# Weights times values of the first network: 64x128 half-array matmuls instead of 64x64 quarters

## Chip, core and metric

The kernel runs on one core of one Trainium2 chip. The metric is the device time of an execution in microseconds; less is better. The core has a matmul engine (TensorE, PE in the profile, with its weight loads listed apart as PEld), VectorE (DVE), ScalarE (ACT), GpSimd (POOL), and a sync engine (SP) that issues most DMAs.

## What is computed

32 records of 64 tokens with 256 dims go through two networks. The first has two cross-attention layers and an MLP; the second is one attention layer and an MLP, and is not touched here. A layer of the first network, cut to what matters:

```python
B, Q, S1, S2 = (4, 32, 256, 256); D, H, K, F = (256, 16, 128, 1024)   # shapes given: batch 32, 64 queries, 64 keys
qh = (q_in @ wq + bq).reshape(b, q_len, H, K)
kh = (kv_in @ wk + bk).reshape(b, t, H, K);  vh = (kv_in @ wv + bv).reshape(b, t, H, K)
kh = concatenate([kh, bias_k]); vh = concatenate([vh, bias_v])       # a 65th key
weights = softmax(einsum('bqhk,bthk->bhqt', qh, kh) / sqrt(K))
ctx = einsum('bhqt,bthk->bqhk', weights, vh).reshape(b, q_len, H * K)
return ctx @ wo + bo
```

The change is in the `ctx` line: per record and head, 64 queries x 64 keys of weights times 64 keys x 128 dims of values.

## The kernel before

Tokens are taken 128 at a time, so that the 128 partitions hold two records (b = 0 on partitions 0 to 63, b = 1 on 64 to 127). A layer is cut into 32 units: 8 pairs of heads (HP) times 4 groups of 512 tokens (G; 4 tiles of 128 tokens, GT). Two layers make 64 units. Each engine runs the same list of slots (`slots`, L248); a slot holds the front of one unit and the back of the unit before it, so a unit is worked on in two successive slots. The order on each engine is written out by hand, and semaphores join the engines.

TensorE's slot (L354 to L453) is, in this order: projections of Q and K (L377, `three`: each product in three fp32r matmuls of 128x128 by 512 columns, L168 to L170); the first half of V, `values(0)` (L387, 12 fp32r matmuls by 256 columns); for the unit before, weights times values (L404); the second half of V, `values(1)`; the scores (L433, plain fp32, stationary QT, moving KT, 65 columns for 64 keys and the bias key); for the unit before, the output projection (L447, 24 fp32r matmuls by 256 columns) of CHI and CLO.

The softmax of a unit lies on VectorE and ScalarE between its scores and its L404 one slot later: maximum (L606), subtraction (L615), exp (L524, ScalarE), sum (L567), reciprocal (L569), product (L571), and eight 32x32-block transposes (L578) that give PRT: 64 keys of record b on partitions b*64 and up, by (head, tile) j, by 64 queries. GpSimd adds to V the difference of bias rows (L332), so that the 65th key needs no row of its own.

The L404 stage: j runs over 8 (2 heads x 4 tiles), b over 2 records. The stationary operand is V (keys of record b x dims of head h), the moving operand is PRT (keys x 64 queries), the result stands in PSUM bank 3 + b, with dims on the partitions and j*64 to (j+1)*64 as columns. Both are plain fp32, which the trace shows as two matmul records and two weight loads per instruction. Before the stage TensorE waits for V (v_shift), PRT (pt_out) and for VectorE to have read banks 3 and 4 (x_settled). Behind it: ScalarE copies each bank to CHI (L513, waits for c_done), VectorE subtracts to get CLO (L596), and the output projection waits for CLO (c_lo). It writes into banks 3 and 4 again; VectorE adds those to X (L625).

Of the kernel before, what the change touches and what calls it, by code (L numbers as in the profile page):

```python
# [13 lines left out]
B, S, D = 32, 64, 256  # L14
TOK = B * S
P = 128
NT = TOK // P
DC = D // P
H, K = 16, 128
# [3 lines left out]
GT = NT // G  # L23
# [21 lines left out]
def program(nc, x, ctx_in, mask, wall, vrow, borow, vech, vecm, b_fc2, qw, kw, vw, ow, out_b, w1, w2, b2, out):  # L45
    es = ExitStack()
    with es:
        def sem(name):
            return es.enter_context(nc.semaphore(name))

        def sb(name, shape, dt=F32, scope=es):
            return scope.enter_context(nc.sbuf_tensor(name, shape, dt))

        bank = [es.enter_context(nc.psum_tensor(f"bank{i}", [P, 512], F32)) for i in range(5)]
# [111 lines left out]
        def three(e, dst, a_hi, a_lo, b_hi, b_lo, start, stop, **kw):  # L166

            e.matmul(dst, a_hi, b_hi, start=start, stop=False, **kw)  # L168
            e.matmul(dst, a_hi, b_lo, start=False, stop=False, **kw)  # L169
            return e.matmul(dst, a_lo, b_hi, start=False, stop=stop, **kw)  # L170
# [16 lines left out]
        with ExitStack() as ph:  # L187
# [13 lines left out]
            V = [sb(f"V{a}", [P, GT, 256], scope=ph) for a in range(2)]  # L201
# [8 lines left out]
            PRT = sb("PRT", [P, 2 * GT, S], scope=ph)  # L210
# [22 lines left out]
            c_done, o_done = sem("c_done"), sem("o_done")  # L233
# [28 lines left out]
            with nc.Block() as block:  # L262
# [90 lines left out]
                def _(e):  # L353
                    def slot(L, n, at, pair, hp, last):  # L354
# [4 lines left out]
                        if front:  # L359
# [6 lines left out]
                            for j, half, done, free in ((0, 1, q_done, v_out), (1, 0, k_done, k_out)):  # L366
# [5 lines left out]
                                for h in range(2):  # L372
# [3 lines left out]
                                    for c in range(DC):  # L376
                                        i = three(e, PROJ[2 * j + h][:, :], WHI[a][:, j, c, h * K:(h + 1) * K],  # L377
                                                  WLO[a][:, j, c, h * K:(h + 1) * K], SRC_HI[:, half, c, toks],
                                                  SRC_LO[:, half, c, toks], c == 0, c == DC - 1)
# [14 lines left out]
                        if back:  # L394

                            e.wait_ge(v_shift, 2 * n)
                            e.wait_ge(pt_out, n)
                            e.wait_ge(x_settled, 2 * n)
                            for j in range(2 * GT):
                                h, p = j // GT, j % GT  # L400
                                for dims in (slice(0, S), slice(S, P)):
                                    for b in range(2):
                                        keys = slice(b * S, (b + 1) * S)
                                        i = e.matmul(bank[3 + b][dims, j * S:(j + 1) * S],  # L404
                                                     V[(at - 1) % 2][keys, p, h * K + dims.start:h * K + dims.stop],
                                                     PRT[keys, j, :], start=True, stop=True)
                                        if j == 2 * GT - 1 and dims.start:
                                            i.then_inc(c_done, 1)
                        if front:
                            values(1)  # L410
                        if at == 0:
# [3 lines left out]
                        if front:  # L415
# [7 lines left out]
                            if last and at == G - 1:  # L423
# [3 lines left out]
                                for c in range(DC):  # L427
                                    e.matmul(logits[:, c, 384:512], ones[:, :], acc[L][:, c * P:(c + 1) * P],
                                             start=True, stop=True)
                            for h in range(2):  # L430
                                for q in range(GTOK // S):
                                    p, b = q // 2, q % 2
                                    i = e.matmul(logits[b * S:(b + 1) * S, h, p * KEYS:(p + 1) * KEYS],  # L433
                                                 QT[:, h, q * S:(q + 1) * S], KT[:, h, q, :], start=True, stop=True)
# [4 lines left out]
                        if back:  # L439

                            e.wait_ge(c_lo, 2 * n)
                            for j in range(2):
                                for p in range(2):
                                    ts = slice((2 * j + p) * P, (2 * j + p + 1) * P)
                                    dst = bank[3 + j][:, p * 256:(p + 1) * 256]
                                    for h in range(2):
                                        i = three(e, dst, CHI[:, h, ts], CLO[:, h, ts], WHI[ab][:, 3, h, :],  # L447
                                                  WLO[ab][:, 3, h, :], h == 0, h == 1)
# [12 lines left out]
                    for g in range(G):  # L461
# [7 lines left out]
                        for c in range(DC):  # L469
                            for p in range(GT):  # L470
                                i = e.transpose(CB[g % 2][c][:, p * P:(p + 1) * P], cin[g % 2][:, p, c * P:(c + 1) * P],
                                                ident[:, :])
# [7 lines left out]
                    for L in range(0, NL):  # L480
                        slots(e, L, slot)
# [849 lines left out]
```

## Time and profile before

| | |
|---|---|
| median of 3 runs | 1415.94 us (1415.51 to 1418.8) |
| profiled execution | 1415.35 us, span 1413.2 us |
| busy: PE | 1334.0 us (94%), 14427 matmul records |
| busy: PEld | 1189.8 us (84%) |
| busy: DVE, ACT, POOL | 904.8 (64%), 611.8 (43%), 587.3 us (42%) |
| L404, matmuls | 4096 records, 76.0 us busy |
| mean granted TensorE clock | 0.976 |

How to read it: the profile is of one execution. The span runs from its first to its last instruction. Busy time of a group of small matmuls is time in which any of them was under way, so overlapping ones aren't counted twice. A matmul record's length includes the time through the array; in a dense stream records overlap, and the distance between their starts is what one costs. A granted clock of 1.00 is 2.4 GHz, 0.50 is 1.2 GHz.

### The profile page before, as it was taken

What the parts mean: (1) busy time and instruction counts of PE and PEld (TensorE: products, weight loads), DVE (VectorE), ACT (ScalarE), POOL (GpSimd) and SP (SyncE); (2) the same over time, 40 slices, a digit from 0 to 9 for tenths busy, and PEclk for the clock granted to TensorE, in tenths of its full rate; (3) what the DMA queues carried; (4) which work ended last, traced back from release to release, by engine and by line L of the source; (5) the groups of instructions that cost most, each with busy time, mean ns of one, the idle gap of its engine ahead of it and who ended that gap; (6) DMA issues with size and microseconds to landing.
All of it is one profiled execution on the core that took longest, in us unless ns stands there. A gap on an engine that the chain in (4) does not pass through costs nothing. (4 is left out here: it accounts for less than half of the span.)

```text
span 1413.2 us, 33171 instructions
## 1 busy us (share of the span) xinstructions
PE 1334.0 (94%) x14427; PEld 1189.8 (84%) x14427; DVE 904.8 (64%) x1792; ACT 611.8 (43%) x1045; POOL 587.3 (42%) x521
## 2 busy tenths in 40 slices
PE   3999999999999799999999999987998999997898
PEld 3898888888888688888888888977887989996787
DVE  6567767676767866767666767685323588886322
ACT  3534343434444554343434444364223256665421
POOL 4524334144144543414414324364651055554654
PEclk8999999999999999999999999997999999998999
DMA  7011011011010101101101011000000000002000
GB/s 241 4 36 39 1 39 39 1 38 39 1 39 2 38 1 39 39 2 38 38 2 39 2 38 38 2 1 27 1 1 8 1 2 2 2 2 64 4 31 30
DMA packets 31764, 35.91 MB, mean 25 GB/s; under 512 B 955, under 2 KB 29187, under 8 KB 31619
## 3 DMA queue, kind: packets, MB, share of 16 engines
q1 hardware_dynamic: 31394, 33.70, 7.6%
q8 instruction: 114, 1.87, 0.6%
q14 instruction: 30, 0.25, 0.1%
q10 hardware_dynamic: 226, 0.10, 0.0%
HBM read 31.70 MB, written 2.10 MB: 24 GB/s over the span
## 5 line engine op out<-in xcount | busy, mean ns | idle before, releaser
L332 POOL TENSOR_TENSOR V<-V,DV 128x512 f32<-128x512 f32 x128 | 164.0, 1281 | 534.5 <-ACT V L500 534.5
L168 PE MATMUL bank<-SRC_HI,WHI 128*128 128x512 f32 x576 | 230.2, 400 | 4.3 <-PEq L262 4.3
L169 PE MATMUL bank<-SRC_LO,WHI 128*128 128x512 f32 x576 | 229.4, 398 | 0.0
L170 PE MATMUL bank<-SRC_HI,WLO 128*128 128x512 f32 x576 | 228.8, 397 | 0.0
L578 DVE STREAM_TRANSPOSE PRT<-PR 32x256 f32<-32x256 f32 x512 | 223.2, 436 | 8.3
L596 DVE TENSOR_TENSOR CLO<-bank,CHI 128x512 fp32r<-128x512 f32 x128 | 82.4, 686 | 135.9 <-ACT CHI L513 135.9
L492 ACT ACTIVATE QT<-bank,PB 128x512 f32<-128x512 f32 x128 | 87.8, 688 | 177.8 <-PE bank L170 177.8
L168 PE MATMUL bank<-WHI,CHI 128*128 128x256 f32 x512 | 152.0, 297 | 4.4 <-DVE CLO L596 4.0
L168 PE MATMUL bank<-WHI,SRC_HI 128*128 128x256 f32 x512 | 150.4, 294 | 0.0
L170 PE MATMUL bank<-WHI,CLO 128*128 128x256 f32 x512 | 145.1, 283 | 0.7 <-issue 0.7
L169 PE MATMUL bank<-WLO,CHI 128*128 128x256 f32 x512 | 144.9, 283 | 0.0
L169 PE MATMUL bank<-WLO,SRC_HI 128*128 128x256 f32 x512 | 143.9, 281 | 0.0
L170 PE MATMUL bank<-WHI,SRC_LO 128*128 128x256 f32 x512 | 143.9, 281 | 0.0
L168 PEld LDWEIGHTS bank<-SRC_HI,WHI 128*128 128x128 f32 x576 | 109.5, 190 | 27.0 <-POOL SRC_LO L163 4.5
L170 PEld LDWEIGHTS bank<-SRC_HI,WLO 128*128 128x128 f32 x576 | 109.2, 190 | 26.4
L169 PEld LDWEIGHTS bank<-SRC_LO,WHI 128*128 128x128 f32 x576 | 109.6, 190 | 21.9
L496 ACT ACTIVATE KT<-bank,PB 128x512 f32<-128x512 f32 x128 | 88.4, 691 | 89.9 <-PE bank L170 89.9
L625 DVE TENSOR_TENSOR X<-X,bank 128x512 f32<-128x512 f32 x128 | 88.0, 687 | 57.9 <-PE bank L170 57.9
L500 ACT ACTIVATE V<-bank 128x512 f32<-128x512 f32 x128 | 76.5, 597 | 79.5 <-PE bank L170 79.5
L168 PEld LDWEIGHTS bank<-WHI,CHI 128*128 128x128 f32 x512 | 98.2, 192 | 9.7 <-DVE CLO L596 5.8
L168 PEld LDWEIGHTS bank<-WHI,SRC_HI 128*128 128x128 f32 x512 | 96.1, 188 | 7.2
L169 PEld LDWEIGHTS bank<-WLO,SRC_HI 128*128 128x128 f32 x512 | 96.5, 188 | 2.7
(170 smaller groups left out, 3009.7 us busy)
## 6 DMA issues: line engine op xcount, KB each, us to landing
W<-in_wall SPq DMA_DIRECT2D x18, 1024.0 KB, 5.6
VROW<-in_vrow SPq DMA_DIRECT2D x18, 256.0 KB, 6.1
V<-in_ctx SPq DMA_DIRECT2D x4, 512.0 KB, 5.8
X<-in_x SPq DMA_DIRECT2D x4, 512.0 KB, 6.8
mlp_w<-in_w SPq DMA_DIRECT2D x2, 1024.0 KB, 7.7
out<-X SPq DMA_DIRECT2D x4, 512.0 KB, 2.9
BO<-in_borow SPq DMA_DIRECT2D x1, 256.0 KB, 7.0
W<-in_qw SPq DMA_DIRECT2D x1, 256.0 KB, 4.3
```

Of the source, the lines that this page charges most:

```text
L168: e.matmul(dst, a_hi, b_hi, start=start, stop=False, **kw)
L169: e.matmul(dst, a_hi, b_lo, start=False, stop=False, **kw)
L170: return e.matmul(dst, a_lo, b_hi, start=False, stop=stop, **kw)
L332: e.tensor_tensor(vs, vs, DV[a][:, :].unsqueeze(1).to_broadcast([P, 2, 2 * K]), ALU.add).then_inc(v_shift, 1)
L492: e.activation(QT[:, h, :], PROJ[h][:, :], ACT.Identity, bias=PB[a][:, 0, h:h + 1]).then_inc(q_out, 1)
L496: e.activation(KT[:, h, :, 0:S], PROJ[2 + h][:, :].rearrange("p (q k) -> p q k", k=S), ACT.Identity, bias=PB[a][:, 1, h:h + 1]).then_inc(k ...
L500: e.activation(V[at % 2][:, 2 * j:2 * j + 2, :], PROJ[j][:, :].rearrange("p (t n) -> p t n", n=256), ACT.Copy).then_inc(v_out, 1)
L578: i = e.transpose(PRT[b * S + z:b * S + z + 32, :, y:y + 32], PR[b * S + y:b * S + y + 32, :, z:z + 32])
L596: e.tensor_tensor(of_batch(CLO, b), by_tile(b), of_batch(CHI, b).bitcast(F32), ALU.subtract).then_inc(c_lo, 1)
L625: e.tensor_tensor(xs, xs, bank[3 + j][:, :].rearrange("p (t n) -> p t n", n=256), ALU.add).then_inc(x_settled, 1)
```

## The change

The loop over two halves of the head dims is gone. One matmul now has all 128 dims of a head in its stationary operand (64 keys x 128 dims) and writes all 128 partitions of the bank. Record b still decides the rows and the bank. So there are 16 instructions a unit (32 records) instead of 32 (64 records). Operands, results, their places in SBUF and PSUM, and all other engines' code are the same; c_done is raised by the last matmul of each b, as before.

```diff
                             for j in range(2 * GT):
                                 h, p = j // GT, j % GT
-                                for dims in (slice(0, S), slice(S, P)):
-                                    for b in range(2):
-                                        keys = slice(b * S, (b + 1) * S)
-                                        i = e.matmul(bank[3 + b][dims, j * S:(j + 1) * S],
-                                                     V[(at - 1) % 2][keys, p, h * K + dims.start:h * K + dims.stop],
-                                                     PRT[keys, j, :], start=True, stop=True)
-                                        if j == 2 * GT - 1 and dims.start:
-                                            i.then_inc(c_done, 1)
+                                for b in range(2):
+                                    keys = slice(b * S, (b + 1) * S)
+                                    i = e.matmul(bank[3 + b][:, j * S:(j + 1) * S],
+                                                 V[(at - 1) % 2][keys, p, h * K:(h + 1) * K],
+                                                 PRT[keys, j, :], start=True, stop=True)
+                                    if j == 2 * GT - 1:
+                                        i.then_inc(c_done, 1)
```

## Rows read from the trace of the kernel before

**Rows 1.** Page: busy us, share of the span and instructions of each engine.

```profile
PE 1334.0 (94%) x14427; PEld 1189.8 (84%) x14427; DVE 904.8 (64%) x1792; ACT 611.8 (43%) x1045; POOL 587.3 (42%) x521
```

**Rows 2.** Windows (us, busy of each engine, then TensorE clock, DMA share, GB/s).

```profile
300.00:400.00 100.00, 99.87 (x1190) 88.73 (x1189) 69.93 (x127) 41.00 (x65) 32.89 (x29) 1.00 0.05 15
485.00:500.00 15.00, 6.97 (x92) 6.62 (x91) 10.98 (x31) 4.67 (x8) 5.33 (x3) 0.66 0.01 1
1200.00:1212.00 12.00, 12.00 (x157) 10.95 (x157) 9.67 (x26) 8.42 (x20) 6.03 (x8) 1.00 0.00 1
```

**Rows 3.** Waits of TensorE, 100:957 (who for whom: us in total, times, longest).

```profile
PE bank L404 <- DVE PRT L578: 12.0, 2, 6.0
...
PE bank L404 <- issue: 1.5, 1, 1.5
```

**Rows 4.** Timeline of TensorE (start us, length us, line, xcount), units at 534 and 548.

```profile
534.43 1.16 PE L404 MATMUL bank<-PRT,V 64*64 64x64 f32 x64
535.52 0.38 PE L168 MATMUL bank<-WHI,SRC_HI 128*128 128x256 f32 x1
...
535.86 0.28 PE L170 MATMUL bank<-WHI,SRC_LO 128*128 128x256 f32 x1
535.98 0.28 PE L168 MATMUL bank<-WHI,SRC_HI 128*128 128x256 f32 x1
...
548.27 1.16 PE L404 MATMUL bank<-PRT,V 64*64 64x64 f32 x64
```

**Rows 5.** By line: ns minimum/median/maximum, starts (x64, x4: 534:537 alone).

```profile
L404 PEld LDWEIGHTS bank<-PRT,V x4096: 129/135/228, 56.0 to 956.2; 64*64 64x64 f32 x196
L404 PE MATMUL bank<-PRT,V x4096: 218/218/366, 56.0 to 956.3; 64*64 64x64 f32 x196
...
L404 PE MATMUL bank<-PRT,V x64: 218/218/267, 534.4 to 535.4; 64*64 64x64 f32 x64
...
L433 PEld LDWEIGHTS logits<-KT,QT x2048: 132/138/138, 46.2 to 944.0; 128*64 128x64 f32 x187
L433 PE MATMUL logits<-KT,QT x2048: 220/222/272, 46.2 to 944.0; 128*64 128x65 f32 x187
...
L1063 PEld LDWEIGHTS bank<-KL,QE x512: 186/192/337, 1133.8 to 1274.5; 128*128 128x128 f32 x171
L1063 PE MATMUL bank<-KL,QE x512: 275/275/421, 1133.8 to 1274.6; 128*128 128x128 f32 x171
...
L1089 PE MATMUL bank<-VS,HT x1024: 202/210/232, 1140.9 to 1279.3; 128*64 128x17 f32 x171
...
L1067 PEld LDWEIGHTS bank<-MA,ONE x64: 100/100/151, 1135.1 to 1274.6; 128*128 128x128 bf16 x64
...
L168 PE MATMUL bank<-WHI,SRC_HI x4: 279/282/384, 535.5 to 536.7; 128*128 128x256 f32 x4
```

**Rows 6.** Timeline of TensorE, groups of small fp32 matmuls.

```profile
537.15 1.15 PE L433 MATMUL logits<-KT,QT 128*64 128x65 f32 x32
...
1201.34 0.65 PE L1089 MATMUL bank<-VS,HT 128*64 128x17 f32 x16
...
1202.09 1.06 PE L1063 MATMUL bank<-KL,QE 128*128 128x128 f32 x8
```

**Rows 7.** Timeline of TensorE, stretches at the lower clock.

```profile
491.57 1.99 PE L404 MATMUL bank<-PRT,V 64*64 64x64 f32 x64 [6.01 <-DVE PRT L578]
...
495.95 0.42 PE L169 MATMUL bank<-WLO,CHI 128*128 128x256 f32 x1
496.16 0.41 PE L170 MATMUL bank<-WHI,CLO 128*128 128x256 f32 x1
...
1135.57 1.91 PE L1063 MATMUL bank<-KL,QE 128*128 128x128 f32 x8
```

**Rows 8.** Timeline of all engines behind the L404 stage of one unit.

```profile
550.12 1.29 DVE L596 TENSOR_TENSOR CLO<-bank,CHI 128x512 fp32r<-128x512 f32 x2 [2.89 <-ACT CHI L513]
...
552.07 0.39 PE L168 MATMUL bank<-WHI,CHI 128*128 128x256 f32 x1
```

## The prediction, made before the changed kernel was run

> **What bounds the kernel now.** First the page: TensorE is busy 1334.0 us of the span of 1413.2, the next engine, VectorE, 904.8 [rows 1]. The windows make this sharper: in the first layer's 300:400 TensorE is busy 99.87 of 100 us at a granted clock of 1.00, VectorE 69.93 [rows 2]. So inside a layer there is no gap on TensorE, and what its instructions take is what the kernel takes. TensorE's own waits say where gaps are: between 100 and 957 us the stage that changes (L404) waited for the transposed weights PRT in two units for 6.0 us each (the last unit of each layer, which has no projections to cover the softmax) and 1.5 us in one other [rows 3]; no other unit of that stretch waits there for any length. The timeline gives a unit's beat, 548.27 - 534.43 = 13.84 us from one L404 stage to the next [rows 4].
>
> Each plain fp32 matmul shows as two records: 32 instructions of the stage are 64 records, 64 units make 4096 [rows 5]. A stage lasts 1.16 us, and the next matmul starts 535.52 - 534.43 = 1.09 us after the stage's first [rows 4]. After the change there are 16 instructions, 32 records, a unit. What decides everything is what one record of the new shape costs, so I look for what limits a record now.
>
> **What limits a small record.** Three groups of small fp32 matmuls, all at full clock [rows 4, 6]; the spacing is (length of the group - one median matmul) over (records - 1), with the medians of [rows 5]:
> - L404, four tiles of 64x64: (1.16 - 0.218)/63 = 15.0 ns a record, so each tile gets one record every 59.8 ns.
> - L433, two column tiles, 128 rows x 64 columns, 65 moving columns: (1.15 - 0.222)/31 = 29.9 ns, each tile one every 59.9 ns.
> - L1089, the same tiles with only 17 moving columns: (0.65 - 0.210)/15 = 29.3 ns, each tile one every 58.7 ns.
>
> L1089 is the telling one: its moving side is a quarter of L433's, and its pace is the same. So the pace isn't set by the moving columns, and 15.0 ns in L404 says that it isn't a fixed cost of a record either. What all three share is a stationary block of 64 columns per tile. The length of a load stands in rows of its own: 135 ns for 64x64, 138 for 128x64, 192 for 128x128 fp32 [rows 5]. Twice the rows: 3 ns. Twice the columns: 54 to 57 ns more. Loads that nothing hides say the same a second way: the first matmul of a group carries its own load, 267 - 218 = 49 ns in L404, 272 - 222 = 50 ns in L433 (64 columns), 384 - 282 = 102 ns in L168 (128 columns) [rows 5]. A tile loads 64 columns in some 50 to 57 ns, different tiles load side by side, and a load runs beside the tile's matmul. In L404 load and matmul are in balance (64 moving columns cost (275 - 218) = 57 ns less than L1063's 128 [rows 5], so some 57 ns too).
>
> The Trainium skill says this as a rule, in "TensorE: Matmul & The Clock Gate", section "LDWEIGHTS (loading the stationary operand)": the load costs the columns of the stationary block over 1.2 GHz, whatever its rows. The trace agrees for 64 against 128 rows (135 and 138 ns) and for the step to 128 columns; by the rule the new load is 107 ns in a tile of its own, 53 ns a record, which speaks against this change.
>
> **The change, part by part.**
> (a) Half the records. The stationary block becomes 64 keys x 128 dims: the same rows, twice the columns. The array then holds two tiles (b = 0 and 1), not four. Weights loaded per tile double, 64 to 128 columns, and each tile still gets 16 records (before 64/4, now 32/2). The moving side stays at 64 columns. No row shows a 64x128 tile. Nearest is L1063, fp32, stationary 128x128, moving 128: (1.06 - 0.275)/7 = 112 ns a record on the full array [rows 6]; its load and its moving side both double those of L404, and 112 is 59.8 x 1.87. If the load limits, a tile of the new shape takes its record every 112 ns, and two tiles side by side give 56 ns a record. The ends: 102 ns, the lone 128-column load above, and 119 ns, the pace of the 128-column loads of L168 to L170 with 256 moving columns (535.98 - 535.86, and 0.12 throughout [rows 4]).
> The new stage, from its first matmul to its last end: 0.218 + 0.102 for the first with its load, then 15 more rounds of 0.112 = 1.68 if both tiles start together, or 31 steps of 0.056 = 1.74 if they alternate: 2.00 to 2.06 us against 1.16. Extra: 0.84 to 0.90, I take 0.87 us a unit. With 102 ns it is 31 x 0.051 + 0.32 - 1.16 = 0.74, with 119 it is 31 x 0.0595 + 0.32 - 1.16 = 1.00.
> (b) Where it lands. TensorE has no gap that could take it up. The stage sits between the two halves of the V projection. In the few units that wait before the stage (PRT, from VectorE), the wait runs from the scores (L433) of the unit before, and no L404 lies between those, so the wait stays as long and the extra comes on top. All 64 count. 62 units at full clock: 62 x 0.87 = 53.9 us.
> (c) The two seam units (491.57 and 954.66 us) run after the 6 us wait with the granted clock at 1.2 GHz for a part; 485:500 has 0.66 [rows 2]. There L404 takes 1.99 us, (1.99 - 0.366)/63 = 25.8 ns a record, 103 ns a tile, and L1063 in its first, slow groups (1.91 - 0.42)/7 = 213 ns a record [rows 5, 7]. New: 15 x 0.213 instead of 15 x 0.103, 1.65 us more each, 3.3 us; at the least 0.87 each as elsewhere. I take 3.
> (d) What hangs on the stage. c_done now comes with the last two records instead of two of the last four, a few tens of ns, and both copies of CHI wait for it as before. Behind it: CLO from 550.12 to 551.41, and the output projection that reads them at 552.07 [rows 8], 0.66 us of slack; the V half (12 records) and the scores between L404 and it are untouched, so this distance stays. ScalarE, VectorE and GpSimd get 0.87 us more per beat of 13.84, work that is the same: their gaps grow. Semaphores, PSUM addresses, DMAs and the order of queues are as before; 2048 fewer matmul records and as many loads cost nothing to leave out, as TensorE is busy without a break inside a layer [rows 2].
>
> Sum: 53.9 + 3 = 57 us. Against the profiled execution (1415.35 us, 2.15 around its span) 1472.4; the median of the runs is 0.6 above it, so I say **1473**. The forecast's own range, 62 x 0.74 + 2 to 62 x 1.00 + 3.3, is 1464 to 1481.
>
> **Rivals.**
> 1. *The new stage takes what the old one did* (1416 us, 10%). It holds if a row group has one load port at about 29 ns for 64 columns: L433 and L1089 fit (29.9 and 29.3 a record), L404's two row groups fit, and 128 columns in each of two row groups would again take 59 ns, 32 x 30 = 0.96 us. Against: the lone loads (49 and 102 ns, not 29 and 59) and the step of 54 to 57 ns in the load's length. Or if the load of a full width is quicker in this mode: the one fast 128-column load in the trace is L1067's, 100 ns long where fp32 takes 192 [rows 5], and with it the 57 ns of the moving side would limit. Against: that one is bf16, and every full-width fp32 load (L1063, L168) is slow.
> The Trainium skill has the rule behind the second way: "TensorEngine Tiling (Array Packing)", section "Restrictions", says that column tiling turns the fast weight load off, and the new shape has no column tiles left; but "TensorE: Matmul & The Clock Gate", section "Weight-path perf modes", grants it only to 128 columns and types other than fp32. The trace agrees on fp32 with L1063's 192 ns.
> 2. *Records cost, not columns* (1387 us, 5%; the other side). If queue and dispatch set 15.0 ns a record, 32 fewer save 32 x 0.015 = 0.48 us less the longer first load of 0.05, 0.43 to 0.48 a unit, 64 x 0.45 = 29 us. It decides as soon as a tile's pace isn't tied to its load. Against: L433 has 32 records and takes as long as L404's 64; L1089 takes 29 ns with almost nothing to stream.
> 3. *The two row tiles don't load side by side* (3%). 112 ns a record, 32 x 0.112 = 3.6 us, +2.5 x 64 = +160, 1576 us. Against: L404 has two row groups and could not reach 15 ns.
> 4. *A part is hidden*, the load starting more than a record ahead so that only 0.3 to 0.7 us shows: 1435 to 1460 us, 4%.
> 5. *The clock falls in the longer, thinner stage* (over 1500 us, 3%): 256-column records go from 0.12 to 0.21 us there [rows 4, 7]. Against: 1200:1212, nearly all small records, stays at 1.00 [rows 2].
> The forecast holds 75%.
>
> **How the numbers follow.** The range is to leave out 2 in 10 at most: 1443 to 1483 holds the forecast with a little for a worse pace, and the upper part of case 4. A change under 0.3% (4 us) can't be told from none here. Faster: case 2 and a sliver of case 1, 6%; same: 8%; slower: 86%.
>
> **What would show it.** L404 in the profile after: 2048 records and 2048 loads of 64x128, the load 185 to 192 ns long, the matmul still 218; the stage 1.9 to 2.1 us; the beat of a unit some 14.7 us; VectorE, ScalarE and GpSimd busy as before to a per cent, their waits for TensorE longer; PE busy about 1390. Wrong would be: a load still near 135 ns (the step in (a) that columns set it), a stage of 1.0 to 1.2 us with loads of 190 (loads more than one deep, or rival 1), a stage of 0.7 (rival 2), or the stage as forecast and the time not moved by 64 times it (b).

## The result and the profile after

The changed kernel takes 1471.54 us (median of 4, 1470.33 to 1473.14) against 1415.76 (median of 4): 1.039 times as long, 95% interval 1.0374 to 1.0407, 55.8 us more. Forecast were 1473 us and a range of 1443 to 1483. The profiled span is 1469.4 us, 56.2 more than before, at a mean clock of 0.974 (before 0.976). One execution each of e1, of e4 and of the kernel before beside e8 was in a slow state (2671.92, 2159.58 and 3505.36 us), and the ratios leave these out.

Engine row of the page after (busy us, share, instructions), to be held against [rows 1]:

```profile
PE 1387.4 (94%) x12379; PEld 1244.4 (85%) x12379; DVE 907.9 (62%) x1792; ACT 612.8 (42%) x1045; POOL 586.5 (40%) x521
```

TensorE has 2048 matmul records less and is busy 53.4 us longer. VectorE has 3.1 us more, the others 1.0 or less: the work of the other engines is what it was. The costliest groups, the stage alone (L403 now; busy us, mean ns of one | idle time before them):

```profile
L403 PE MATMUL bank<-PRT,V 64*128 64x64 f32 x2048 | 131.5, 279 | 19.0 <-DVE PRT L577 13.8
L403 PEld LDWEIGHTS bank<-PRT,V 64*128 64x128 f32 x2048 | 123.1, 192 | 28.7 <-issue 22.6
```

and its durations (ns minimum/median/maximum), which answer to the L404 rows of [rows 5]:

```profile
L403 PEld LDWEIGHTS bank<-PRT,V x2048: 182/188/335, 56.6 to 1010.5; 64*128 64x128 f32 x187
L403 PE MATMUL bank<-PRT,V x2048: 272/272/472, 56.7 to 1010.6; 64*128 64x64 f32 x187
```

The load of 64x128 is 188 ns long, near the 192 of a 128x128 load; that of 64x64 was 135. The matmul record is 272 ns, not 218, though its moving side is the same 64 columns. In the middle of a stage its record now begins 132 ns before its load's record ends, where it was 79 ns before: 53 ns more, the length by which the load grew. The stage of one unit and the next unit's start, timeline of TensorE, against [rows 4]:

```profile
563.14 2.00 PE L403 MATMUL bank<-PRT,V 64*128 64x64 f32 x32
565.07 0.38 PE L168 MATMUL bank<-WHI,SRC_HI 128*128 128x256 f32 x1
...
577.82 2.00 PE L403 MATMUL bank<-PRT,V 64*128 64x64 f32 x32
```

The stage is 2.00 us instead of 1.16, the next matmul starts 1.93 us after its first instead of 1.09, and the unit's beat is 577.82 - 563.14 = 14.68 us instead of 13.84. The pace in the stage is (2.00 - 0.272)/31 = 55.7 ns a record, 111.5 ns for each of two tiles; before it was 15.0 and 59.8. This formula spreads the longer first record, which carries its own load, over all the others. The starts in the trace show the pace itself: in the middle of a stage a tile's next record follows after 112 ns (median over the stages); before it was 58 ns. I call that time a round. The window in the first layer, against [rows 2]:

```profile
300.00:400.00 100.00, 99.72 (x922) 89.20 (x923) 64.96 (x119) 39.12 (x62) 33.65 (x32) 1.00 0.09 27
```

TensorE is busy 99.72 us of 100, at full clock; VectorE does 64.96 us of work in 100 instead of 69.93. The waits of the others for TensorE (total us, times, longest) show where the 0.84 us went on their side:

```profile
DVE CLO L595 <- ACT CHI L512: 186.4, 60, 4.4
ACT QT L491 <- PE bank L170: 177.0, 121, 2.3
...
ACT CHI L512 <- PE bank L403: 101.3, 60, 9.4
```

ScalarE waits 101.3 us for the stage to finish (48.3 before) and VectorE 186.4 us for CHI (135.9 before), 0.84 us a wait each (60 waits). Both had time to spare.

The seam units, at the lower clock, against [rows 7]:

```profile
517.61 3.68 PE L403 MATMUL bank<-PRT,V 64*128 64x64 f32 x32 [6.90 <-DVE PRT L577]
```

3.68 us instead of 1.99, and TensorE waits 6.90 us for PRT ahead of it instead of 6.01.

### The profile page after: what moved, and what is told of

It is laid out like the page before. It is cut to its first block and busy times, and to the rows that moved or that the text cites. A ratio compares the mean times of both kernels' runs of the same rounds, so it can differ in the third digit from the quotient of the medians.

```text
span 1469.4 us, 29075 instructions
## 1 busy us (share of the span) xinstructions
PE 1387.4 (94%) x12379; PEld 1244.4 (85%) x12379; DVE 907.9 (62%) x1792; ACT 612.8 (42%) x1045; POOL 586.5 (40%) x521
## 5 line engine op out<-in xcount | busy, mean ns | idle before, releaser
L595 DVE TENSOR_TENSOR CLO<-bank,CHI 128x512 fp32r<-128x512 f32 x128 | 82.4, 686 | 186.4 <-ACT CHI L512 186.4
L403 PE MATMUL bank<-PRT,V 64*128 64x64 f32 x2048 | 131.5, 279 | 19.0 <-DVE PRT L577 13.8
L403 PEld LDWEIGHTS bank<-PRT,V 64*128 64x128 f32 x2048 | 123.1, 192 | 28.7 <-issue 22.6
L168 PEld LDWEIGHTS bank<-SRC_HI,WHI 128*128 128x128 f32 x576 | 109.7, 190 | 27.2 <-POOL SRC_LO L163 4.5
L512 ACT ACTIVATE CHI<-bank 128x512 fp32r<-128x512 f32 x128 | 69.4, 594 | 101.3 <-PE bank L403 101.3
```

Source lines behind the costliest of these rows:

```text
L403: i = e.matmul(bank[3 + b][:, j * S:(j + 1) * S], V[(at - 1) % 2][keys, p, h * K:(h + 1) * K], PRT[keys, j, :], start=True, stop=True)
L512: e.activation(of_batch(CHI, b), by_tile(b), ACT.Copy).then_inc(c_hi, 1)
L595: e.tensor_tensor(of_batch(CLO, b), by_tile(b), of_batch(CHI, b).bitcast(F32), ALU.subtract).then_inc(c_lo, 1)
```

## The experiments

The theory after the result, with the figures I had then: a tile takes its next record after the longer of two things, the load of its stationary block and the stream of its moving columns, both some 53 ns for 64 fp32 columns and 107 for 128; tiles of the array go side by side. The change doubled the load in each tile and left the number of records per tile. Rivals: a load port per row group; a fixed cost of a record; a moving side that costs a half-array tile double; a sum of both sides. In what follows "pace" is (length of the group - one median matmul) over (records - 1). That formula averages over the whole stage; where it misleads, the round is read from the starts in the trace. All timed kernels ran beside the kernel before (medians 1415.5 to 1416.5).

### e1: quarters, two tiles in use at a time

```diff
-for j in range(2 * GT):
-    for dims in (slice(0, S), slice(S, P)):
+for dims in (slice(0, S), slice(S, P)):
+    for j in range(2 * GT):
         for b in range(2):
```

> The kernel before, its 64 records of 64x64 a unit, with the loop over the two halves of the dims outermost, so that for half of the stage only the two tiles of one column half are in use (record b = 0 and 1, two row groups). Nothing else changes. Theory (a load takes about 57 ns per 64 columns in the tile that it loads, tiles side by side): two tiles share the pace, 30 ns a record instead of 15, stage 0.22 + 0.05 + 63 x 0.030 = 2.1 us instead of 1.16, 64 x 0.93 = +60 us, 1472 to 1476. Rival 1 (one load port per row group at 29 ns for 64 columns): both row groups stay busy, 15 ns a record, 1416, no change. Rival 2 (a record costs 15 ns): 1416 too.

1465.2 us (three executions at 1463.77 to 1466.17; the median has the fourth in it), ratio 1.0344 (1.0326 to 1.0361). Timeline, the stage of two units:

```profile
572.58 1.91 PE L404 MATMUL bank<-PRT,V 64*64 64x64 f32 x64
...
587.17 1.91 PE L404 MATMUL bank<-PRT,V 64*64 64x64 f32 x64
```

The pace is (1.91 - 0.218)/63 = 26.9 ns on average. The same 64 records with the same blocks cost 0.75 us more in a unit, only because two of four tiles stood idle in each half. With a load port per row group nothing could have changed, as both row groups were busy throughout; with a fixed cost of a record neither. Both rivals are out. The round of a tile is 58 ns (median), the same as with four tiles: a tile's pace is its own, however many others are at work. My size was 7 us too high for another reason. The 26.9 ns are an average over the switch from one half of the dims to the other, where the two halves use different tiles. In the stage at 572.58 the second half's first records start 761 and 767 ns in, and the first half's last ones some 925 ns in: about three rounds overlap. That is 3 x 0.058 = 0.17 us of 64 stages, 11 us, and I had counted none.

### e2: halves, one tile in use at a time

```diff
-for j in range(2 * GT):
-    h, p = j // GT, j % GT
-    for b in range(2):
+for b in range(2):
+    for j in range(2 * GT):
+        h, p = j // GT, j % GT
```

> The changed kernel with the loop over b outermost, so that 16 records go to the one 64x128 tile and then 16 to the other: no two tiles in use at once. Theory (a tile takes 112 ns for a 128-column load, the two tiles side by side in the changed kernel): 112 ns a record, stage 0.32 + 31 x 0.112 = 3.8 us instead of 2.00, +1.8 x 64 = +115, 1580 to 1590. If the tiles already took turns in the changed kernel (a shared load port at 56 ns for 128 columns, or a cost of 56 ns a record): no change, 1471.

1620.99 us, ratio 1.1464 (1.1431 to 1.1497): the way is the forecast one, the size isn't. A stage in an undisturbed unit:

```profile
468.55 3.39 PE L403 MATMUL bank<-PRT,V 64*128 64x64 f32 x32
```

3.39 us against 2.00 in the changed kernel: 1.39 more, 64 x 1.39 = 89 us. A tile's round is 112 ns (median), the same as with two tiles side by side, so in the changed kernel the two tiles did load side by side. That the stage isn't 3.8 us is again the switch: the second tile starts 1395 ns in, while the first one's last record starts 1725 ns in, three rounds later. But the spans differ by 1615.5 - 1469.4 = 146 us, 57 more than 89. The windows around another stage (busy of each engine, then the clock) say why:

```profile
431.86 3.39 PE L403 MATMUL bank<-PRT,V 64*128 64x64 f32 x32
```

```profile
430.00:432.00 2.00, 2.00 (x16) 1.77 (x15) 0.80 (x2) 0.72 (x2) 0.00 (x0) 1.00 0.00 0
432.00:434.00 2.00, 2.00 (x23) 2.00 (x23) 0.00 (x0) 0.67 (x2) 1.26 (x1) 1.00 0.00 0
434.00:436.00 2.00, 2.00 (x16) 1.93 (x15) 0.77 (x2) 1.09 (x2) 0.00 (x0) 0.80 0.00 0
436.00:438.00 2.00, 2.00 (x10) 1.81 (x9) 0.61 (x1) 0.00 (x0) 0.00 (x0) 0.50 0.00 0
```

The granted clock is 1.00 during the stage and falls to 0.50 right behind it, and the projections after it run at 1.2 GHz. The beat is 16.1 us in quiet units and above 16.6 in 35 of 63. The kernel's mean clock is 0.932. Between the first stage and the last the granted clock is 0.50 for 151 us, in the changed kernel for 16. If TensorE went at half its rate in the 135 us more, that would cost 68 us, an estimate from above that has room for the 57. This is rival 5 of the prediction, met not by the changed kernel's 2.00 us stage but by one of 3.39 us with mostly one tile at work. That the 57 us are this and nothing else, and that it is the thin stage that the clock answers to, was not shown by a run of its own.

### e3 and e4: half the moving columns

The other 32 queries of each block are left out.

```diff
-bank[3 + b][..., j * S:(j + 1) * S], V[...], PRT[keys, j, :]
+bank[3 + b][..., j * S:j * S + 32], V[...], PRT[keys, j, 0:32]
```

> The changed kernel with 32 of the 64 queries as moving columns; the other half of each block is left out. Loads are as they were. Theory (the loads set the pace): no change but for some ns on the last record, 1469 to 1472. Rival (a half-array record pays for its moving columns at half rate, so 64 cost 107 ns a tile): half of it goes, pace 30 ns, 64 x 0.8 = -51, 1420. Rival that the pace is the sum of load and moving side: 0.027 x 16 x 64 = -27, 1444.

> The kernel before with 32 of the 64 queries as moving columns; the other half is left out. Theory (64-column loads take some 53 to 57 ns a tile, which the moving side only matches): at most 1 to 2 ns per tile and round, as L1089 with 17 moving columns (58.7 against 59.8 ns a tile): 1412 to 1416. If the moving columns set the pace of the quarters: 30 ns a tile, stage 0.5 us shorter, 64 x 0.45 = -29, 1387.

e3 (halves): 1469.01 us, ratio 1.0378 (1.0362 to 1.0393). e4 (quarters): 1416.27 us, ratio 1.0001 (0.9992 to 1.0011). A stage of each:

```profile
580.77 1.98 PE L403 MATMUL bank<-PRT,V 64*128 64x32 f32 x32
```

```profile
574.61 1.14 PE L404 MATMUL bank<-PRT,V 64*64 64x32 f32 x64
```

The halves keep 1.98 us with half the stream, (1.98 - 0.273)/31 = 55 ns a record: the load alone sets their pace. The rivals by which the moving columns set or share it (1420 and 1444) are out. The quarters keep 1.14 us, and a round of 58 ns as before: there too half of the stream brings nothing. By e4 alone the 58 ns could also be four records at a fixed cost of 14.5; but in e1 two tiles have the same round of 58 with half as many records in it. So the 58 ns are the tile's own, and its load's. (e4's time is 0.3 us above its forecast of 1412 to 1416.)

### e5 and e6: twice the moving columns

```diff
-bank[3 + b][..., j * S:(j + 1) * S], V[...], PRT[keys, j, :]
+m = min(j, 2 * GT - 2)
+bank[3 + b][..., m * S:(m + 2) * S], V[...], PRT[keys, m:m + 2, :]
```

> The changed kernel with 128 moving columns in each matmul of the stage (two neighbouring blocks of weights at once; the results written are not those of the product wanted). Loads as in the changed kernel. Theory (a record costs a tile the larger of its load, some 107 ns for 128 columns, and its moving side, some 107 ns for 128 fp32 columns): the doubled moving side is free but for the last record, +0.06 x 64 = 4, 1472 to 1478. If load and moving side add up in a tile: +16 x 0.053 x 64 = +54, 1525.

> The kernel before with 128 moving columns in each matmul of the stage (results again not those wanted), loads of 64 columns as before. Theory (the larger of the two sides): now the moving side limits, 107 to 112 ns a tile, 28 ns a record, stage 2.0 to 2.1 us instead of 1.16, +56 to +60, 1470 to 1477, as slow as the changed kernel with twice its loads. If only loads ever set the pace: 1416 to 1420.

e5 (halves): 1473.52 us, ratio 1.0401 (1.0383 to 1.042), 2 us above the changed kernel. e6 (quarters): 1468.38 us, ratio 1.0366 (1.0349 to 1.0382). A stage of each, and e6's durations:

```profile
581.02 2.06 PE L404 MATMUL bank<-PRT,V 64*128 64x128 f32 x32
```

```profile
575.02 1.98 PE L405 MATMUL bank<-PRT,V 64*64 64x128 f32 x64
...
L405 PE MATMUL bank<-PRT,V x4096: 269/269/471, 55.2 to 1007.4; 64*64 64x128 f32 x196
```

With a 128-column load a 128-column stream is free, 2.06 us against 2.00; with a 64-column load the same stream adds 0.82 us, and the pace is (1.98 - 0.269)/63 = 27.2 ns, 109 ns a tile, which is also the round in the trace. So the larger side decides, and they don't add. Quarters with twice the stream cost nearly what halves with twice the load cost (e6 came out 1.6 us below its forecast of 1470 to 1477). The lengths of the records go by the larger side too: 218 ns with 64 columns on both, 269 with 128 moving, 272 or 273 with a load of 128 and 32, 64 or 128 moving. The two runs also hold the change itself once more, under a stream of 128: there it costs 2.06 - 1.98 = 0.08 us a stage instead of 0.84.

### e7: halves in the first layer, quarters in the second

```diff
+if L == 0:
     (the 16 half-array matmuls)
+else:
     (the 32 quarter-array matmuls)
```

> The changed stage in the 32 units of the first layer, the stage of before in the 32 of the second. Theory (each unit pays by itself, nothing is absorbed or given back elsewhere): half of the difference, 1416 + 28 = 1442 to 1446. If a part came from a cost once per kernel or from the second layer alone: off from the middle by more than 4 us.

1445.61 us, ratio 1.0207 (1.0185 to 1.0229), 29.1 us more, about half of 55.8. A unit of each layer:

```profile
336.35 2.00 PE L404 MATMUL bank<-PRT,V 64*128 64x64 f32 x32
...
576.02 1.16 PE L415 MATMUL bank<-PRT,V 64*64 64x64 f32 x64
```

The cost belongs to the unit that has the shape, and stays there.

### e8: quarters in crossed order

```diff
-for dims in (slice(0, S), slice(S, P)):
-    for b in range(2):
+for b, lo in ((0, 0), (1, S), (0, S), (1, 0)):
```

> A try for a faster stage: the kernel before with its four 64x64 tiles in another order, so that neighbouring instructions differ in rows and, for two of three steps, in columns too. Two tiles alone took 53.7 ns a round against 59.5 with all four in use, so something small is lost among four. Theory (the pace is the tile's own load, with a little lost to tiles that share rows): at best 16 x 4 ns x 64 = -4 us, 1412; more likely no change, 1414 to 1418. If the order between rows and columns mattered for loads side by side at all (as it would with one load port per row group), the stage would move by tenths of a microsecond: over 10 us either way.

1415.14 us, ratio 0.9997 (0.9985 to 1.0008): no change.

```profile
575.73 1.16 PE L403 MATMUL bank<-PRT,V 64*64 64x64 f32 x64
```

Once all four tiles are fed, this change of their order doesn't matter. The premise of the try was wrong: it set 53.7 ns for two tiles against 59.5 for four, and by the starts in the traces a round is 58 ns in both, so there was nothing to win. No experiment points to a shape faster than the one before.

## Why the prediction was right, and where its steps were off

(a) *Half the records, twice the load in each tile.* Right. I put 112 ns a tile and 56 ns a record, from the full-array L1063; measured 111.5 and 55.7 by the same formula, and a round of 112. The stage was put at 2.00 to 2.06 us and is 2.00; the extra was taken as 0.87 us and is 0.84, the value for both tiles starting together. The load's length was as said. The matmul's 218 ns was wrong (272): a record's length grows with its load, as if it held the time in which it waits for it (a reading, not tested). That touches a step of the working. I had taken L1063's 275 ns against 218 as the price of 64 more moving columns; the changed kernel has 272 ns without them, so these rows could not tell stream from load. e6 can: 269 ns for a stream of 128 with a load of 64. So a long stream does cost what I said, but the row I gave didn't show it. And the 59.8 ns a tile that I read for L404 is the average with the first record in it, where the round is 58.

(b) *No gap takes it up, all 64 count.* Right for nearly all: from the first L404 to the last, 63 beats, the starts go from 56.04 and 954.66 to 56.66 and 1007.38, 52.1 us more, where 63 x 0.84 would be 52.9. Wrong in one full unit and part of a second, the ones before the seams. There TensorE waits for the layer norm's XN (L137), with VectorE and not TensorE as the bound. Timeline of TensorE, before and after:

```profile
466.02 1.09 PE L137 MATMUL bank<-ident,XN 128*128 128x128 f32 x8 [2.20 <-DVE XN L128]
```

```profile
490.84 1.09 PE L137 MATMUL bank<-ident,XN 128*128 128x128 f32 x8 [1.35 <-DVE XN L128]
```

The wait shrinks from 2.20 to 1.35 us and the beat is 17.3 us in both kernels: the 0.84 us are absorbed. I had looked at the waits ahead of the stage itself, not at one behind it in the same slot. Its row stands in the view of [rows 3], between the two shown there:

```profile
PE bank L137 <- DVE XN L128: 2.2, 1, 2.2
```

In the second layer's twin the beat grows by 0.29 (15.24 to 15.53). Another 1.0 us lies in the kernel before: one of its units, at 590.02, takes 14.81 us, with a gap of 0.66 on TensorE at 596.77 that nothing in the profile accounts for, and the changed kernel's profile has no such unit; what caused it stays open.

(b), second half: *the wait for PRT stays as long.* Wrong by 0.9 us at each seam (6.01 to 6.90 at the first), of which only a part reaches the time: the first such beat grows from 14.29 to 15.49 us, 0.36 more than the stage. VectorE's product PR, just ahead of the transposes, took 0.69 us before:

```profile
487.15 0.69 DVE L571 TENSOR_TENSOR PR<-ex,ri 128x512 f32<-128x512 f32 x1
```

and 1.58 us after, beside two instructions of GpSimd (VectorE, then GpSimd):

```profile
512.31 1.58 DVE L570 TENSOR_TENSOR PR<-ex,ri 128x512 f32<-128x512 f32 x1
...
510.74 2.60 POOL L163 TENSOR_TENSOR SRC_LO<-HT,SRC_HI 128x512 fp32r<-128x512 f32 x2 [3.00 <-ACT SRC_HI L152]
```

GpSimd's subtraction L163 ends at 513.34 and the product at 513.89, 0.55 us later, as if it had waited for it. The two traces bear this out: the product takes over 1.5 us in 16 of 64 units before and in 19 after (1852 ns at most in both), each time beside a GpSimd instruction that had started before it or within 16 ns, and ends 0.55 us behind that one. Where the product starts clearly first, by 0.09 us at 487.15, it takes 0.69 us, and it is GpSimd's L163 beside it that takes 1.76 us instead of some 1.3. So it is how the two engines' instructions happen to meet, which the change has shifted; read from the traces only, not tested by a run. The Trainium skill says in "SBUF — State Buffer", section "SBUF: two separate sides", that VectorE and GpSimd share a port pair that one of them holds for a whole instruction. These rows agree.

(c) *The seam units.* 1.65 us more each expected, 1.69 measured (3.68 against 1.99). With the longest record of the row above, (3.68 - 0.472)/31 = 103.5 ns a record, 207 a tile, against 213 expected.

(d) *What hangs on the stage.* Right: VectorE, ScalarE and GpSimd only wait longer, and no new wait on TensorE appears behind the stage.

Sum: 57 us forecast against 1415.35, 56.2 between the spans. The parts: 0.6 at the start, 52.1 over the 63 beats, 3.5 from the last stage on, of which 1.7 is the stage itself. The other 1.8 is the net of waits in the part behind the first network, above all that for swap at the head of the second (4.66 us instead of 2.92); why it grew was not traced. The terms off (0.03 us too much a unit, some 1.4 us absorbed before the seams, 1.0 in that one unit of the kernel before, against what the new waits add) nearly cancel: that the sum comes within 1 us of the measured one is in that part luck, while the 0.84 us a stage is not. Of the rivals, 1 fell by e1 (the port per row group) and by the load's length of 188 ns (the quicker load), 2 by e1, 3 and 4 by the stage itself, 2.00 us (and 3 by e2 once more); 5 didn't happen in this kernel.

## What to carry to other kernels

Count per tile of the array, not per instruction: in these runs, at full clock, a tile's next plain fp32 record came after the larger of its load and its stream. The load took 58 ns a round for 64 columns and 112 for 128, the stream 109 for 128 (and for 64 no more than the load's 58). That, times the records of a tile, is nearly the whole stage. Joining column tiles into one wide block halves the instructions but doubles the load in the tile, and so costs time where the load is already the larger side (0.84 us a stage here); it is nearly free where the moving side is as long as the new load (0.08 us, e5 against e6). The order of instructions must keep all tiles fed (e1, e2).

## What the runs showed of the hardware that was not expected

- The clock can fall though TensorE is never idle: with mostly one 64x128 tile at work for 3.39 us (e2) the granted clock went from 1.00 to 0.50 behind the stage in about half of the units. Their beat was mostly some 17.5 us instead of 16.1, so such a stage cost about as much behind it (1.4 us) as in it. In the changed kernel's profile, with two such tiles for 2.00 us, no unit inside a layer has this. It isn't ruled out there: in e7's profile the clock is at 0.50 from 56.5 to 59.9 us, just as the first unit's stage of this kind (54.77 us) ends.
- The round of a tile doesn't depend on how many tiles are at work: 58 ns for 64x64 with two tiles and with four, 112 ns for 64x128 with one tile and with two. An average over a stage hides this where the stage goes from one set of tiles to another, because about three rounds of the old and the new tiles overlap there.
- A matmul record's length goes by the larger of its load and its stream: 218 ns became 272 with the wider load alone, and 269 with the longer stream alone.
- VectorE's two-input product and GpSimd's instructions took turns: where GpSimd's had started first or at the same moment, the product took 1.58 to 1.85 us instead of 0.69 (35 of 128 units in the two traces); where the product had, GpSimd's took 1.76 instead of 1.3.
